# The last five blocks of the first FFN pass in three fp32r products

## The reference

```python
h = _L0_tok_ref(x, L0_tok_W, L0_tok_b)                  # 64 x 10 x 512
h = h + _L0_attn_ref(_layernorm(h, axis=-1), Wq, Wk, Wv, Wo)   # 16 heads, 10 positions, heavy-key and band mask
h = h + _L0_ffn_ref(_layernorm(h, axis=-1), w_gate_up, w_down)

# the feed-forward network (FFN), 512 -> 2 x 2048 -> 512:
gate_up = jnp.einsum('bsh,oh->bso', h_shard, w_gate_up)
gate, up = jnp.split(gate_up, 2, axis=-1)
out = jnp.einsum('bsi,hi->bsh', jax.nn.silu(gate) * up, w_down)
```

## Time and profile before

| | |
|---|---|
| median of 3 runs | 285.42 us (284.55 to 286.07) |
| the profiled execution | 284.75 us |
| its span in the profile | 282.8 us |
| busy: PE, DVE, ACT, POOL | 273.1, 161.6, 79.5, 53.0 us |
| first pass, from its first matmul | 71.99 us |
| second pass, from its first matmul | 175.58 us |

### The profile page before, as it was taken

The page is one execution under the profiler, slowest core; times in us unless marked ns, Lnnn a source line. Parts: engine busy times, 40 slices in busy tenths (PEclk is TensorE's granted clock), DMA queues, the critical chain, the costliest instruction groups (busy, mean ns, idle before and its releaser), DMA issues.

```text
span 282.8 us, 4587 instructions
## 1 busy us (share of the span) xinstructions
PE 273.1 (97%) x1781; PEld 215.7 (76%) x1781; DVE 161.6 (57%) x312; ACT 79.5 (28%) x148; POOL 53.0 (19%) x41
## 2 busy tenths in 40 slices
PE   7999999999799999999999999999999999999994
PEld 6555486683687867767865667899999999999992
DVE  1676998995779998669704535453333443333313
ACT  2311214520510112350101123243344443433330
POOL 0104000010024510007300001052222223322210
PEclk9999999999999999999999999999999999999999
DMA  7994030000005334534403023385444333330003
GB/s 229 416 415 135 1 114 2 2 2 0 1 16 197 124 114 127 205 113 148 188 0 111 23 92 121 127 312 184 135 137 167 117 111 111 111 111 0 0 0 111
DMA packets 6815, 32.76 MB, mean 116 GB/s; under 512 B 976, under 2 KB 976, under 8 KB 6288
## 3 DMA queue, kind: packets, MB, share of 16 engines
q1 hardware_dynamic: 6512, 32.15, 32.4%
q10 hardware_dynamic: 288, 0.39, 0.4%
HBM read 31.23 MB, written 1.31 MB: 115 GB/s over the span
## 4 chain that ended last, share of the span: by engine, by line
PE 93%; DVE 2%; ACT 2%; issue 1%; POOL 0%; DVEq 0%; POOLq 0%
PE ps L210 36%; PE ps L1075 18%; PE ps L1085 10%; PE ps L952 5%; PE ps L1014 5%; PE ps L1006 4%; PE ps L930 4%; PE ps L967 3%; PE ps L957 3%; PE ps L883 2%; PE ps L1019 1%; PE ps L936 1%; PE ps L994 1%; ACT v_all L395 1%; PE ps L887 1%
## 5 line engine op out<-in xcount | busy, mean ns | idle before, releaser
L210 PE MATMUL ps<-xT,wgu 128*128 128x384 f32 x384 | 70.9, 340 | 0.1
L210 PEld LDWEIGHTS ps<-xT,wgu 128*128 128x128 f32 x384 | 68.1, 188 | 2.5 <-DVE xT L577 0.9
L1075 PE MATMUL ps<-whole,stage 128*128 128x256 f32 (+1 forms) x288 | 58.3, 357 | 1.0 <-ACT whole L362 1.0
L1075 PEld LDWEIGHTS ps<-whole,stage 128*128 128x128 f32 x288 | 49.6, 190 | 11.7 <-issue 4.8
L790 DVE TENSOR_TENSOR gu<-silu,ps 128x256 f32<-128x256 f32 (+1 forms) x32 | 15.5, 484 | 67.7 <-PE ps L210 44.8
L303 POOL TENSOR_TENSOR wd<-stage,wd 128x512 fp32r<-128x512 f32 x16 | 26.8, 1675 | 78.7 <-ACT wd L362 78.7
L210 PE MATMUL ps<-wd,hT 128*128 128x512 f32 x144 | 35.7, 393 | 0.0
L467 ACT ACTIVATE silu<-ps 128x256 f32<-128x256 f32 (+1 forms) x32 | 14.0, 438 | 75.0 <-PE ps L1075 48.6
L210 PEld LDWEIGHTS ps<-wd,hT 128*128 128x128 f32 x144 | 26.8, 188 | 5.0
L1085 PE MATMUL ps<-stage,gu 128*128 128x512 f32 x64 | 30.1, 592 | 0.0
L362 ACT ACTIVATE wgu<-stage 128x1024 fp32r<-128x1024 f32 x16 | 16.9, 1058 | 22.6 <-PE ps L210 20.9
(11 more groups left out here) (100 smaller groups left out, 252.0 us busy)
## 6 DMA issues: line engine op xcount, KB each, us to landing
stage<-w_ffn SPq DMA_DIRECT2D x32, 768.0 KB, 4.3
stage<-w_k SPq DMA_DIRECT2D x1, 1024.0 KB, 6.7
stage<-w_q SPq DMA_DIRECT2D x1, 1024.0 KB, 10.1
stage<-w_v SPq DMA_DIRECT2D x1, 1024.0 KB, 12.2
wo<-w_o SPq DMA_DIRECT2D x1, 1024.0 KB, 13.8
out<-ob SPq DMA_DIRECT2D x14, 64.0 KB, 2.3
const<-consts SPq DMA_DIRECT2D x1, 800.0 KB, 8.1
out<-ob ACTq DMA_DIRECT2D x6, 64.0 KB, 1.9
```

Of the source, the lines that this page charges most:

```text
L210: ins = pe.matmul(dst, lhs[a], rhs[b], start=first and n == 0, stop=last and n == 2)
L1075: ins = pe.matmul(ps[:, bank, at + a:at + b], stage[:, slot, w:w + P], xf[:, k, a:b], start=k == 0, stop=k == KT - 1)
```

## The change

For blocks 11 to 15 of the first pass (NS = 5, S0 = 11), `gate_up_whole` and `down_whole` use `mm3` on halves. The tokens of tiles 0 and 1 get halves once, in a new buffer `xs`; weights and gated units of each of the five blocks get halves in the rings that the second pass uses later. ScalarE makes the high halves, VectorE the low ones, those of `wd` too. GpSimd's own low halves stay as they were, for the second pass. All counts of the shared semaphores in the second pass rise by NS. VectorE's value products of the last unit are regrouped.

```diff
+NS = 5
+S0 = NB - NS
+        xs = sb("xs", [P, 2, KT, 2 * P], F32R)
 # ScalarE
+            def hi_whole():
+                act.wait_ge(xf_sb, 2)
+                split_hi(xs[:, 0], xf, xs_hi)
+            def hi_weights(i):
+                slot, ring = i % SLOTS, i % 2
+                act.wait_ge(dma_stage[slot], stage_count(A, i, slot))
+                if i >= S0 + 2:
+                    act.wait_ge(gu_mm[A], 2 * (i - 1))
+                split_hi(wgu[:, ring, 0], stage[:, slot, 0:2 * KT * P], wgu_hi)
+                if i >= S0 + 2:
+                    act.wait_ge(down_mm[A], i - 1)
+                hi_down(i, ring, slot)
             def first_pass(i):
                 silu_gate(A, i, i % 2)
+                if i >= S0:
+                    act.wait_ge(gu_prod[A], i + 1)
+                    split_hi(hT[:, i % 2, 0, 0:2 * P], gu[:, i % 2, 0:2 * P], hT_hi)
...
             exponential(5)
+            hi_whole()
             for i in range(9, 12):
+                if i + 1 >= S0:
+                    hi_weights(i + 1)
                 first_pass(i)
             hi_attn(3)
             hi_attn(4)
+            hi_weights(13)
             first_pass(12)
             hi_attn(5)
             hi_xT(LN2[2])
+            hi_weights(14)
             first_pass(13)
             hi_xT(LN2[4])
+            hi_weights(15)
             first_pass(14)
             hi_gu(0, 0, 0)
             hi_xT(LN2[3])
             first_pass(15)
+            act.wait_ge(down_mm[A], NB - 1)
             hi_down(0, 0, 0)
 # VectorE
+            def low_whole():
+                dve.wait_ge(xs_hi, 1)
+                dve.tensor_tensor(xs[:, 1], xf, f32(xs[:, 0]), ALU.subtract).then_inc(xs_lo, 1)
+            def low_weights(i):
+                slot, ring = i % SLOTS, i % 2
+                lo_gu(i - NB, ring, slot)
+                dve.wait_ge(wd_hi, i - S0 + 1)
+                dve.tensor_tensor(wd[:, ring, 1], stage[:, slot, 2 * KT * P:FW], f32(wd[:, ring, 0]), ALU.subtract).then_inc(wd_lo, 1)
+            def low_units(i):
+                dve.wait_ge(hT_hi, i - S0 + 1)
+                dve.tensor_tensor(hT[:, i % 2, 1, 0:2 * P], gu[:, i % 2, 0:2 * P], f32(hT[:, i % 2, 0, 0:2 * P]), ALU.subtract)\
+                   .then_inc(hT_lo, 1)
...
             values(1, 9)
+            low_whole()
+            low_weights(11)
             first_pass(10)
-            values(1, 6, 5, 3)
+            values(1, 6, 5)
+            low_weights(12)
             first_pass(11)
-            values(1, 2, 1, 0)
+            low_units(11)
+            values(1, 3, 2, 1, 0)
+            low_weights(13)
             first_pass(12)
+            low_units(12)
             statistics(LN2[2])
             normalise(LN2[2])
+            low_weights(14)
             statistics(LN2[4])
             first_pass(13)
+            low_units(13)
             low(LN2[2])
             normalise(LN2[4])
+            low_weights(15)
             statistics(LN2[3])
             first_pass(14)
+            low_units(14)
             low(LN2[4])
             normalise(LN2[3])
             lo_gu(0, 0, 0)
             low(LN2[3])
             first_pass(15)
+            low_units(15)
 # TensorE, gate_up_whole
+                if i >= S0:
+                    pe.wait_ge(xs_lo, 1)
+                    pe.wait_ge(wgu_lo, i - S0 + 1)
+                    for up, (bank, at) in enumerate((GATE[A][ring], UP[A][ring])):
+                        for k in range(KT):
+                            w = D * up + P * k
+                            ins = mm3(pe, ps[:, bank, at + a:at + b], [wgu[:, ring, n, w:w + P] for n in range(2)],
+                                      [xs[:, n, k] for n in range(2)], k == 0, k == KT - 1)
+                        ins.then_inc(gu_mm[A], 1)
+                    return
 # TensorE, down_whole
-                pe.wait_ge(gu_prod[A], i + 1)
+                if i >= S0:
+                    pe.wait_ge(hT_lo, i - S0 + 1)
+                    pe.wait_ge(wd_lo, i - S0 + 1)
+                else:
+                    pe.wait_ge(gu_prod[A], i + 1)
                 for u in range(TILES[A]):
+                    if i >= S0:
+                        ins = mm3(pe, ps[:, DOWN[A][u], :], [hT[:, i % 2, n, P * u:P * (u + 1)] for n in range(2)],
+                                  [wd[:, i % 2, n] for n in range(2)], False, last)
```

More of the change, by code:

```diff
@@ L199, in audio_tower @@
         wgu_hi, wgu_lo, wd_hi, wd_lo, hT_hi, hT_lo = (sem(n) for n in ("wgu_hi", "wgu_lo", "wd_hi", "wd_lo", "hT_hi", "hT_lo"))
-        dve_step, xf_sb = sem("dve_step"), sem("xf_sb")
+        dve_step, xf_sb, xs_hi, xs_lo = (sem(n) for n in ("dve_step", "xf_sb", "xs_hi", "xs_lo"))
         def repeated(ap, dim, n):
@@ L290, in _ @@
                 for u in range(SLOTS):
-                    sp.wait_ge(wgu_lo, SLOTS * n + (u + 1))
-                    sp.wait_ge(wd_lo, SLOTS * n + (u + 1))
+                    sp.wait_ge(wgu_lo, SLOTS * n + (NS + u + 1))
+                    sp.wait_ge(wd_lo, SLOTS * n + (NS + u + 1))
                     sp.dma_start(stage[:, u, 0:FW], w_ffn[bass.ds(SLOTS * n + (SLOTS + u), 1)].rearrange("o p n -> (o p) n"))\
@@ L328, in lo_down @@
             def lo_down(i, ring, slot):
-                pool.wait_ge(wd_hi, i + 1)
+                pool.wait_ge(wd_hi, i + (NS + 1))
                 low(wd[:, ring, 1], stage[:, slot, 2 * KT * P:FW], wd[:, ring, 0], wd_lo)
@@ L477, in second_pass @@
                     act.wait_ge(gu_mm[Z], 2 * i + 2)
-                    act.wait_ge(wgu_lo, i + 1)
+                    act.wait_ge(wgu_lo, i + (NS + 1))
                     hi_gu(i + 2, ring, (u + 2) % SLOTS)
@@ L486, in second_pass @@
                         act.wait_ge(down_mm[Z], i)
-                        act.wait_ge(wd_lo, i)
+                        act.wait_ge(wd_lo, i + NS)
                     hi_down(i + 1, 1 - ring, (u + 1) % SLOTS)
@@ L777, in lo_gu @@
             def lo_gu(i, ring, slot):
-                dve.wait_ge(wgu_hi, i + 1)
+                dve.wait_ge(wgu_hi, i + (NS + 1))
                 dve.tensor_tensor(wgu[:, ring, 1], stage[:, slot, 0:2 * KT * P], f32(wgu[:, ring, 0]), ALU.subtract)\
@@ L799, in second_pass @@
                 up_product(Z, i, ring)
-                dve.wait_ge(hT_hi, i + 1)
+                dve.wait_ge(hT_hi, i + (NS + 1))
                 dve.tensor_tensor(hT[:, ring, 1], gu[:, ring], f32(hT[:, ring, 0]), ALU.subtract).then_inc(hT_lo, 1)
@@ L1069, in gate_up_whole @@
                 slot, ring = i % SLOTS, i % 2
+                a, b = P * tiles[0], P * tiles[-1] + P
+                if i >= S0:
[8 more added lines that the diff above has]
+                    return
                 pe.wait_ge(dma_stage[slot], stage_count(A, i, slot))
-                a, b = P * tiles[0], P * tiles[-1] + P
                 for bank, at in (GATE[A][ring], UP[A][ring]):
@@ L1080, in down_whole @@
             def down_whole(i):
-                pe.wait_ge(gu_prod[A], i + 1)
                 last = i == NB - 1
-                for u in range(TILES[A]):
-                    ins = pe.matmul(ps[:, DOWN[A][u], :], gu[:, i % 2, P * u:P * (u + 1)], stage[:, i % SLOTS, 2 * KT * P:FW],
-                                    start=i == 0, stop=last)
+                if i >= S0:
[3 more added lines that the diff above has]
+                    pe.wait_ge(gu_prod[A], i + 1)
+                for u in range(TILES[A]):
+                    if i >= S0:
+                        ins = mm3(pe, ps[:, DOWN[A][u], :], [hT[:, i % 2, n, P * u:P * (u + 1)] for n in range(2)],
+                                  [wd[:, i % 2, n] for n in range(2)], False, last)
+                    else:
+                        ins = pe.matmul(ps[:, DOWN[A][u], :], gu[:, i % 2, P * u:P * (u + 1)], stage[:, i % SLOTS, 2 * KT * P:FW],
+                                        start=i == 0, stop=False)
                     if last:
@@ L1098, in gate_up @@
             def gate_up(i, ring):
-                pe.wait_ge(wgu_lo, i + 1)
+                pe.wait_ge(wgu_lo, i + (NS + 1))
                 for up, (bank, col) in enumerate((GATE[Z][ring], UP[Z][ring])):
@@ L1110, in down @@
             def down(i, ring, first=False, last=False):
-                pe.wait_ge(hT_lo, i + 1)
-                pe.wait_ge(wd_lo, i + 1)
+                pe.wait_ge(hT_lo, i + (NS + 1))
+                pe.wait_ge(wd_lo, i + (NS + 1))
                 for u in range(TILES[Z]):
```

## The result

The changed kernel took 301.35 us (median of 4 runs, 299.46 to 302.1) against 285.47 for the kernel before (median of 4 runs): slower, ratio 1.0549, 95% interval 1.0488 to 1.0611. The forecast was 299.0, range 294.5 to 303.5. The profiled execution took 300.63 us (span 298.4) against 284.75 (282.8).

The account below looks back on a forecast made before the run. TensorE, holding 93% of the chain, was taken to bound the kernel: 284.75 us profiled, -4.15 products, +7.2 first wait, +2.0 clock, +8.7 three waits, +0.33 last turn = 298.85, forecast at 299.0, range 294.5 to 303.5.

Parts of the forecast that it names:

- the clock's term: In the gap before gate/up 11 TensorE's granted clock falls, and its return costs 2.0 us; ends 0 and 4.
- a rival at 0.09: The clock falls in later gaps also, each fall costing up to 2 us more: 301 to 303 us; chance 0.09.
- The first wait: Gate/up 11 waits for the low half of block 11's weights on VectorE and starts 7.2 us late; bounds 3.1 and 8.
- the shift by ScalarE's copy: hi_whole, between exponential(5) and the table load with silu(9), makes VectorE's and GpSimd's value work start 1.03 us later.
- GpSimd's turns: Before gate/up 11, VectorE operations on two SBUF tensors stand still while GpSimd multiplies, and the reverse; GpSimd's three products span 7.47 us.
- The rival without this standing still: VectorE and GpSimd don't hold each other up: first wait 3 to 4 us, clock holds, 293.5 us; chance 0.04.
- The three waits: Before transposes LN2[2], LN2[4] and LN2[3], ScalarE's wd split waits for down(i-2): 2.0, 3.1 and 3.6, together 8.7 us.
- The pitch: fp32r matmuls of 256 columns take 0.123 us: gate/up 2.95 us, down 1.39, five blocks 4.15 us off TensorE.
- the likeliest case: The forecast itself, 299.0 us, with one clock fall of 2.0 us at the first wait; chance 0.65.
- The last turn: Between transposes LN2[3] and the second pass, down 14 covers 1.39 us in place of 1.72: 0.33 of its gain lost.

Follow-up runs that it names:

- the kernel with memory of its own: Changed kernel, with the down weights' halves of blocks 13, 14 and 15 in memory of their own, so ScalarE's copies wait for no down: 292.87 us, ratio 1.0261.
- TensorE's part alone: Kernel before, with gate/up and down of blocks 11 to 15 as three fp32r products on halves ScalarE fills once, early, from other data: 280.56 us, ratio 0.9838.
- tokens' copy early: Changed kernel, with ScalarE's copy of the tokens after silu of block 4 in place of right behind exponential(5): 298.12 us (one run).
- TensorE kept busy: Changed kernel, with seven fp32 matmuls of 512 columns, results never read, on TensorE ahead of the wait for block 11's halves: 298.99 us, ratio 1.0525.
- GpSimd's value products later: Changed kernel, with GpSimd's second and third of its last three value products waiting until VectorE has block 11's low half: 299.51 us, ratio 1.0453.
- later split: Changed kernel, with the wd split for blocks 13 to 15 later on ScalarE and VectorE, and statistics(4) and (3) ahead of gate/up's low half: 290.14 us, ratio 1.0179.

## Why the prediction was right

The forecast of 299.0 was 2.35 us low, and its terms and their places hold; the one clear miss is the size of the clock's term. The measured median lies inside the stretch of 301 to 303 us that the prediction gave to a rival at 0.09, so the mechanism was that rival's in part.

- **The first wait.** Predicted 7.2 us, measured 7.16 late (7.00 idle). Its parts hold too: the shift by ScalarE's copy (predicted 1.03, 0.93 in the timeline, 0.9 when taken away) and GpSimd's turns (1.82 + 1.16 = 3.0 expected before that run, 2.9 when taken away). The rival without this standing still falls.
- **The three waits.** Predicted 2.0, 3.1 and 3.6; TensorE idled 1.73, 2.91 and 3.52, and by the starts of its groups the transposes were 1.89, 3.07 and 3.68 late (1.55 + 0.34, 2.73 + 0.34, 2.71 + 0.63 + 0.34, the table's difference plus what the products save in the stretch): 8.64 in all against 8.7. The mechanism is the one named, ScalarE's wait for down, with silu queued behind it and the LayerNorm behind that on VectorE, and the kernel with memory of its own shows its share (5.8 of 8.2).
- **The pitch.** Predicted 0.123 us, from the slope between 384 and 512 columns; measured 0.1175. Gate/up is 2.82 and not 2.95, down 1.38 and not 1.39, so the five blocks take 4.85 us off TensorE in place of 4.15. Less the last turn's 0.34 that is 4.5; the kernel with TensorE's part alone gained 4.7, where 3.8 was expected.
- **The clock.** The fall was foreseen and its place also; its size was low. Predicted 2.0 us in all. At the first wait it cost 2.4 (5.26 against 2.90), and the clock fell again behind the wait of 3.52 us, which the prediction had as a rival with 0.09: second pass to the end is 0.75 longer where down 15 alone should make it 0.34 shorter, so about 1.1. The reading behind this term doesn't hold as a measure. The prediction saw the clock fall 3.5 to 4 us after TensorE's end and so held waits of 3.1 and 3.6 us for hardly long enough; in the first wait of the changed kernel it fell 2.1 us after the last matmul, and behind the wait of 3.52 us 1.5 us after work had begun again. The profiled execution is 1.8 us above the sum of 298.85; by the table these are +1.5 of clock, +0.8 at the start, +0.3 around the span, and -0.7 for products that are cheaper than predicted. So part of the nearness of 299.0 is luck: the clock's excess and the cheaper products have opposite signs. The spread of the runs goes with the clock too: 299.46 us at a mean granted clock of 0.980, 302.1 at 0.972. So the likeliest case and the rival "it falls in later gaps also" came together in this kernel.
- **The last turn.** Predicted 0.33 lost of down 14's gain, measured 0.4 of wait in every version that has no other; right. It is the whole gain of down 14 (0.34): the stretch from transposes LN2[3] to the second pass is 2.39 us in the kernel before and in the one with TensorE's part alone.

## What to carry to other kernels

When work moves to engines that look half idle, read the queue at each insertion: what is behind the new instruction, what does it wait for, and who waits for that. Here nearly the same instructions (one subtraction went from VectorE to GpSimd) cost 15.9 us in one order and gained 3.8 in another. A copy into a ring buffer whose slot comes free late belongs as late in its queue as its reader allows. And a gap on TensorE is priced with its clock's return, not by its length alone.

## What the runs showed of the hardware

- When GpSimd's and VectorE's operations on two SBUF tensors were both queued, they took turns: a VectorE subtraction of 1024 elements took 2.98 and 2.31 us beside GpSimd's products and 1.21 with none in its way.
- fp32r matmuls with a weight load each go at 0.1175 us for 256 columns, 0.177 for 384 and 0.231 for 512 (the last in the second pass of the kernel before; in blocks of six, 1.38/6 = 0.230). The step from 256 to 384 columns (0.060 us) is larger than from 384 to 512 (0.054), which a straight line had not foreseen.
- The granted clock fell in or behind each profiled wait of TensorE of 3.5 us and more (3.52, 3.61, 4.15, 6.07 and 7.0), and came back only when TensorE had worked for some time again (5.2 us at the first wait of the changed kernel, 3.9 where the wait was 6.07). Behind the same wait of 2.91 us it held in three executions (changed kernel, tokens' copy early, TensorE kept busy) and fell in one (GpSimd's value products later), after work had begun again. In the waits of 7.0 us of three kernels it fell 2.1, 2.4 and 4.7 us after the last matmul (changed kernel, halves in memory of their own, later split). So neither the moment of a fall nor the price of a gap near 3 us is fixed.
- In the timeline the first fp32r matmul after an fp32 one is recorded some 0.4 us early: gate/up 12 in TensorE's part alone starts at 144.76 and its down at 147.89, 3.13 us, where gate/up 13, behind transposes, has 2.82. Its end is not late. A duration is better read from the start of the next group.
